# Two-layer graph attention on one core: the norms subtract the mean itself, without an array of negated means

## The reference, cut to what matters

```python
def layer_norm(x, g, b):
    m = jnp.mean(x, axis=-1, keepdims=True)
    v = jnp.mean(jnp.square(x - m), axis=-1, keepdims=True)
    return (x - m) * jax.lax.rsqrt(v + LN_EPS) * g + b
...
x = layer_norm(x + ctx, ln_g[k], ln_b[k])                       # k = 0, 1
...
return (y - mu) * jax.lax.rsqrt(var + EPS) * gamma + beta       # the eight-head layer
```

## Time and profile before

| | |
|---|---|
| median of three runs | 1194.66 us (1193.97 to 1195.53) |
| the profiled execution: time / span | 1193.67 us / 1191.8 us |
| PE busy | 1151.6 us, 97% of the span |
| DVE busy | 975.9 us, 82% |
| ACT busy | 927.7 us, 78% |
| POOL busy | 543.1 us, 46% |
| chain that ended last | PE 90%, DVE 5%, ACT 2%, issue 2%, DMA 1%, POOL 1% |

### The profile page before, as it was taken

How to read it: one execution, slowest core, us unless ns; L and a number is a source line. 1 busy time by engine, 2 the same in 40 slices (tenths; PEclk the granted TensorE clock), 3 DMA queues, 4 the chain that set the end, 5 groups by cost and what they waited for, 6 DMA issues and landing times.

```text
span 1191.8 us, 28469 instructions
## 1 busy us (share of the span) xinstructions
PE 1151.6 (97%) x9596; PEld 840.7 (71%) x9596; DVE 975.9 (82%) x2680; ACT 927.7 (78%) x2115; POOL 543.1 (46%) x410
## 2 busy tenths in 40 slices
PE   7988999999999999999999999999999999999796
PEld 4656777777777777777777777777777777777463
DVE  5877888898888888888888888888888888888776
ACT  5436888878888787888878888887888888788774
POOL 2561346434544644354454435545443564444330
PEclk9899999999999999999999999999999999999999
DMA  8024261614425152431615234260532516122411
GB/s 230 19 77 102 70 144 37 180 35 125 90 70 162 37 152 63 121 93 47 185 35 145 72 88 126 37 196 19 142 90 72 143 37 182 32 74 74 113 27 36
DMA packets 164446, 112.48 MB, mean 94 GB/s; under 512 B 100944, under 2 KB 146000, under 8 KB 164304
## 3 DMA queue, kind: packets, MB, share of 16 engines
q1 hardware_dynamic: 162144, 102.80, 33.6%
q0 software_dynamic: 2160, 7.87, 1.9%
HBM read 61.87 MB, written 25.17 MB: 73 GB/s over the span
## 4 chain that ended last, share of the span: by engine, by line
PE 90%; DVE 5%; ACT 2%; issue 2%; DMA 1%; POOL 1%; DVEq 0%; POOLq 0%; ACTq 0%; SPq 0%
PE ps_j L868 40%; PE ps_t L881 23%; PE ps_j L1008 10%; PE ps_s L860 8%; PE ps_s L854 7%; ACT probs L1068 1%; PE ps_j L1016 1%; DVE masked_s L1169 1%; DMA xt<-ys 1%; PE ps_j L975 1%; DVE y_l L1288 0%; POOL ys L674 0%; DMA x<-x_dram 0%; DVE stats_L L1189 0%; PE ps_j L1034 0%
## 5 line engine op out<-in xcount | busy, mean ns | idle before, releaser
L1169 DVE CUSTOM_DVE_ANT_0 masked_s<-ps_s,mask 128x512 f32<-128x512 f32 x640 | 424.8, 681 | 21.8 <-PE ps_s L860 21.6
L1068 ACT ACTIVATE probs<-masked_s,nm_h 128x512 f32<-128x512 f32 x512 | 367.3, 718 | 73.3 <-DVE nm_h L1169 66.8
L881 PE MATMUL ps_t<-ident,probs 128*128 128x128 f32 x2560 | 390.5, 275 | 6.7 <-ACT pt_h L1074 3.0
L881 PEld LDWEIGHTS ps_t<-ident,probs 128*128 128x128 f32 x2560 | 305.5, 142 | 86.8 <-issue 23.2
L1074 ACT ACTIVATE pt_h<-ps_t 128x512 f32<-128x512 f32 x401 | 236.2, 589 | 77.3 <-PE ps_t L881 72.5
L860 PE MATMUL ps_s<-stack 128*128 128x512 f16 x512 | 194.5, 381 | 2.6 <-DVE nm_h L1169 2.6
L868 PE MATMUL ps_j<-xw,pt_l 128*128 128x256 f16 x1536 | 189.1, 274 | 1.8 <-DVE parts L1347 1.0
L868 PEld LDWEIGHTS ps_j<-xw,pt_l 128*128 128x128 f16 x1536 | 150.8, 98 | 32.9 <-DVE pt_l L1204 2.1
L656 POOL TENSOR_TENSOR rstd_L<-var_eps_L,minus_half 128x4 f32<-128x4 f32 x32 | 32.8, 1025 | 220.8 <-DVE var_eps_L L1199 220.8
L1008 PE MATMUL ps_j<-pt_h,v 128*32 128x256 f32 x2048 | 123.6, 382 | 2.7 <-DVE pt_h L1176 2.4
L1204 DVE TENSOR_TENSOR pt_l<-ps_t,pt_l 128x512 f16<-128x512 f32 x128 | 88.3, 690 | 30.1 <-ACT pt_l L1074 20.8
(11 more groups left out here) (143 smaller groups left out, 1640.0 us busy)
## 6 DMA issues: line engine op xcount, KB each, us to landing
stack<-bounce SPq DMA_DIRECT2D x256, 128.0 KB, 3.0
bounce<-parts SPq DMA_DIRECT2D x64, 256.0 KB, 2.6
adj_t<-adj_dram SPq DMA_DIRECT2D x30, 512.0 KB, 5.4
x<-x_dram SPq DMA_DIRECT2D x16, 512.0 KB, 3.9
out_dram<-y_f POOLq DMA_DIRECT2D x15, 512.0 KB, 3.4
stack<-adj_dram SPq DMA_DIRECT2D x2, 512.0 KB, 5.7
pt_h<-l_wc SPq DMA_DIRECT2D x2, 256.0 KB, 4.8
out_dram<-y_f SPq DMA_DIRECT2D x4, 128.0 KB, 1.8
```

What stands on the lines that cost most here:

```text
L881: last = pe.transpose(ps_t[r % 2][:, t], probs[:, r, t * P:(t + 1) * P], ident[:])
L1068: act.activation(probs[:, r], masked_s[:, r], ACT.Exp, bias=nm[:, n, r:r + 1], scale=-1.0, accum_out=total[:, n, r:r + 1]).then_inc(exps, 1)
L1169: dve.tensor_tensor_reduce(out=masked_s[:, r], in0=ps_s[scores_bank(pos)][:], in1=m[:, r], scale=-scale, scalar=NONE_LEFT, op0=ALU.add, op ...
```

## The change

The array `minus_mean` and the instruction that fills it go. The three places that read it now read the mean from `moments`, and their first operation is a subtraction instead of an addition. Nothing else is changed; the waits and the order of the rest stay.

```diff
-        minus_mean = {s: sb(f"minus_mean_{s}", [P, NT]) for s in "LF"}
...
# POOL, finish
-                    last = pool.tensor_scalar(y_f[:, t], y_f[:, t], minus_mean["F"][:, t:t + 1],
-                                              rstd["F"][:, t:t + 1], ALU.add, ALU.mult)
+                    last = pool.tensor_scalar(y_f[:, t], y_f[:, t], moments["F"][:, t, 0:1],
+                                              rstd["F"][:, t:t + 1], ALU.subtract, ALU.mult)
...
# DVE, statistics
-                    dve.tensor_scalar(minus_mean[s][:], moments[s][:, :, 0], -1.0, None, ALU.mult)
                     dve.tensor_reduce(var_eps[s][:], moments[s][:, :, 1:3], ALONG, ALU.add)\
                         .then_inc(moments_ready[s], 1)
...
# DVE, job N
-                        last = dve.tensor_scalar(y[:, t], y[:, t], minus_mean["L"][:, t:t + 1],
-                                                 rstd["L"][:, t:t + 1], ALU.add, ALU.mult)
+                        last = dve.tensor_scalar(y[:, t], y[:, t], moments["L"][:, t, 0:1],
+                                                 rstd["L"][:, t:t + 1], ALU.subtract, ALU.mult)
...
# DVE, the last graph
-                dve.scalar_tensor_tensor(y_f[:, t], y_f[:, t], minus_mean["F"][:, t:t + 1], gain[:, 2],
-                                         ALU.add, ALU.mult).then_inc(normed["F"], 1)
+                dve.scalar_tensor_tensor(y_f[:, t], y_f[:, t], moments["F"][:, t, 0:1], gain[:, 2],
+                                         ALU.subtract, ALU.mult).then_inc(normed["F"], 1)
```

## The result

| | before | after |
|---|---|---|
| median | 1193.97 us (11 runs) | 1197.51 us (11 runs) |
| ratio | | 1.0023, 95% interval 1.0015 to 1.0032 |
| span of the profiled execution | 1191.8 us | 1195.7 us |
| POOL busy | 543.1 us | 584.0 us |
| DVE busy | 975.9 us | 969.8 us |

So the change makes the kernel 2.7 us slower by the ratio (0.0023 x 1194; 1.8 to 3.8 us by its interval). Two of the 11 runs (1230.19 and 1716.69 us, at a lower granted clock) are in the median but not in the ratio.

A forecast was written before the change was run, and what follows sets the result against it. PE bounds the loop, so only prologue and tail can shorten: 0.18 + 0.07 + 0.08 + 0.16 = 0.5 us, with POOL's subtraction at nothing. Forecast 1194.66 - 0.5 = 1194.2 us, range 1192.9 to 1197.2.

The forecast's parts named there:

- what changes in place: Reads and operations that stay: DVE's subtraction costs nothing; POOL's in finish taken as nothing, 548 ns an instruction.
- The argument from two-input operations: On POOL, two-input subtraction is no dearer (1024 elements: add 2366, mult 2364 ns; 512: subtract 1161), so finish pays nothing.
- The rule: POOL bodies of up to two operations run at port rate, so subtraction in finish is free: sum stays -0.5 us.
- The bounds: POOL's (subtract, mult) in finish: 548 ns if quick, 923 if slow in one pass, 1511 at twice the slow slope.
- The same, dearer: Rival, 15%: POOL's subtraction costs 1.1 to 1.51 us each; tail +2.2 to +3.9 us, net +1.7 to +3.4.
- The sign: If wrong: POOL's row at 900 ns or more, both PE waits of the tail longer by four times the difference.
- the saving of 0.18 us: Start of the tail: rstd comes 0.10 us earlier behind POOL's copy, which itself moves 0.08 us; shortens PE's waits.
- The limit of 2.1 us a norm: Loop: rstd passes 617.06, where y_l starts, only from +2.1 us a norm on; until then its delay is free.
- The 10.3 us of DVE: DVE time given back by the 48 removed instructions: 11.9 + 2.7 - 48 x 0.09 us, overlaps taken off.
- the 14.6 us named as a sign: If right: DVE busy some 14.6 us lower over the kernel.
- The waits for POOL (6.4 us): Some 6.4 of the 10.3 us: removed L instructions stretched beside POOL's copy, waits that leave with them.
- The small gains: Savings on the path: tail's start 0.18 us, last F norm 0.07, the one before 0.08, prologue 0.16; sum 0.5.

The follow-up runs named there:

- price list: Kernel before plus 24 GpSimd instructions on scratch behind its last one, to price operation pairs; at 256 elements (add, mult) 551 ns, (subtract, mult) 1220 ns.
- graph 13 alone: Kernel before with (subtract, mult) on GpSimd only in the F norm of graph 13, the one ahead of the tail; ratio 1.0021.
- VectorE's part alone: Kernel before without the negated means of the 32 L norms and the last F norm; GpSimd keeps (add, mult) with the other 15; ratio 0.9992.
- all but graph 13: Kernel before with (subtract, mult) on GpSimd in the 14 F norms of finish other than graph 13's; ratio 1.0009.
- VectorE's part with another order: Kernel before, negated means gone only where VectorE reads them; at the tail's start GpSimd makes rstd and split rows before the residual's copy; ratio 0.9995.

## Why the prediction was wrong

- **The step that failed** is in the part on what changes in place: "so I take nothing, from the row nearest in form (L749 itself)". The price of (subtract, mult) on POOL was the one open term, I had seen in the earlier trace rows that POOL has a quick and a slow way, and chose the quick one; it was the slow one, 1215 ns. The argument from two-input operations, where subtraction isn't dearer, doesn't carry over to this form. What stood in the sum at nothing was 4 x 0.667 = 2.67 us at the start of the tail. A reader of the earlier trace rows should have given the slow way the greater chance: two of the three tensor_scalar forms in them were slow, both single operations, and a pair that isn't shown is no more like the quick one than like those.
- **The rule against the rows.** By the Trainium skill, GPSIMD Engine Reference, section 3.1, a body of up to two operations runs at the port's 1.03 cycles per element; by the clock of 1.2 GHz that the page uses, that is an estimate of 0.86 ns. The prediction weighed it against the earlier trace rows and left it undecided. The price list decides: the rule fits (add, mult), with 0.84 ns per element, and the two pairs that cost the same at 256 elements, but not the six other forms with per-partition scalars, which cost 920 to 1230 ns there.
- **The bounds.** 548 to 1511 ns held the price. The upper one was worked out with twice the slope of a single operation, 4.6 ns per element; measured were 3.3. That slope came from a row with a per-partition value and one with a constant, and the two aren't priced alike: (subtract, mult) takes 1220 ns with the one and 1076 ns with the other.
- **The rival** *The same, dearer* had the mechanism and the place right, at 15%. It gave +2.67 - 0.5 = +2.2 us for 1215 ns; the ratio says +2.7, for graph 13 alone +2.5. Its time, 1196.4 to 1198 us, held the measured 1197.51. That rival put the point for a loss above 0.2% at 1.27 us an instruction; at 1.215 us the measured loss is already 0.23%, though its interval also holds the rival's 2.2 us. The range ended at 1197.2, 0.3 us short: it took in only the lower part of this case.
- **The sign.** The prediction would have seen both PE waits of the tail longer by four times the difference. Only the first is, by 2.5 us. When y_l comes later, the first wait already moves PE by as much, so the wait for the DMA behind it needn't grow; here it shrank, because the matmuls in front of it ran slower. For the same reason the saving of 0.18 us could show in one of the two only, and in VectorE's part alone it does: the first wait is 2.26 us in place of 2.44 us, the second 2.33 us as before.
- **The loop.** The limit of 2.1 us a norm, up to which a later rstd is free, held: at 2.67 us DVE waited for rstd in each of the 13 other bodies, (13.2 - 3.60)/13 = 0.74 us on average, where less than 1 us was worked out; in four of them, whose store landed late, it was 1.16 to 1.45 us. That PE has room behind it isn't quite so: the kernel with all but graph 13 is 0 to 0.18 per cent slower, and its profile shows one wait of 0.6 us for a DMA.
- **The 10.3 us of DVE** were 6.1 us (and the 14.6 us named as a sign counted the overlaps twice). The waits for POOL (6.4 us) did go: var_eps takes 0.16 us in each place. But the 0.08 us of an undisturbed instruction mostly weren't there to have. Where the masking of scores (masked_s) comes next, it is 0.19 us from var_eps, now first behind the aggregates, to that instruction, and it was 0.19 us from minus_mean to it with var_eps between them (600.35 to 600.54). Why isn't shown. Where another instruction comes next, the time does come back: 0.08 us in place of 0.15 us behind the prologue's norm at 59.94. DVE's timeline after, which answers to the earlier trace rows:

```profile
600.91 0.16 DVE L1197 TENSOR_REDUCE var_eps_F<-moments_F 128x4 f32<-128x8 f32 x1
601.10 0.69 DVE L1168 CUSTOM_DVE_ANT_0 masked_s<-ps_s,mask 128x512 f32<-128x512 f32 x1
```

- **The small gains** that do lie on a path are right in size as far as they can be seen: at the end it is 0.28 us from var_eps (1189.74) to the next row instruction (1190.02), where it was 0.34 us from minus_mean (1185.75, 1186.09), 0.06 us against the 0.07 us of the forecast. VectorE's part, in which nearly all of them are, measured 0.9 us (-0.1 to 2.0), where 0.5 us were forecast; the interval holds the forecast and also nothing.

What stays open is how much the loop costs over many executions (0 to 2.1 us by the interval), and why the prologue takes one of two courses that differ by up to 1.7 us; each course was seen with the prologue of the kernel before and with that of the kernel after. Only profiled executions show the course, so its share in the ratios isn't known.

## What to carry to other kernels

On GpSimd the pair of operations of an instruction is part of its price: before an algebraically equal form replaces one in use, look for a row of that very pair, and if there is none, take the slow price as at least as likely. An array that seems superfluous (16 instructions of 0.17 us here) can be what keeps another engine's instructions on a quick way. And when an engine that is busy half of the time gets more work, the question isn't its share but what its queue holds next: here 4 instructions of 60 made most of the loss, and it went when the norm's rstd no longer stood behind the wait for the store and one copy.

## What the runs showed of the hardware

- GpSimd, fp32, 256 elements, per-partition scalars: 548 to 556 ns for (add, mult), (mult, add), (mult, mult); 920 to 924 ns for any single one of add, subtract, mult; 1215 to 1230 ns for (subtract, mult), (mult, subtract), (add, add). Two operations can be quicker than one.
- VectorE's four-element multiplication by a constant waited for the end of a GpSimd copy (0.60 us in place of 0.17); a four-element reduction in its place didn't (0.16 us). The timelines of DVE and POOL of VectorE's part alone show it inside a running copy:

```profile
614.36 0.16 DVE L1200 TENSOR_REDUCE var_eps_L<-moments_L 128x4 f32<-128x8 f32 x1
...
613.95 1.03 POOL L742 COPY y_f<-x 128x1024 f32<-128x1024 f32 x1 [2.80 <-DMA out_dram<-y_f]
```

  By the Trainium skill, SBUF — State Buffer, section "Who interferes with whom", copies and tensor_scalar can enter a mode that takes the port pair shared with GpSimd, and reductions can't; the trace agrees for the multiplication (0.60 us) and for the reduction (0.16 us).
- PE's 32 matmuls behind a wait of 4.89 us took 3.59 us at a granted clock of 0.51, and behind 2.44 us they took 1.93 us at 1.00. In the prologue, six matmuls took 2.74 us behind a wait of 3.78 us (clock 0.50), and 1.47 us behind one of 2.11 us (1.00). The length of the wait just before doesn't decide it alone: six matmuls behind 2.35 us took 2.74 us in VectorE's part with another order, and 1.47 us behind 2.33 us before; the 32 took 2.64 us behind 2.50 us in all but graph 13.
